# First layer's scan: high and low part of x in one 128-row operand, one selection product per tile

## The reference

```python
Bm = x @ W_B.T + b_B;  Cm = x @ W_C.T + b_C                  # 16 states
Delta = softplus(x @ W_Delta.T + b_Delta + bias_Delta)
A_bar = exp(A * Delta)                                       # [t, 256, 16]
B_bar = 1 / A * (A_bar - 1) * Bm
state = state * A_bar + x[..., None] * B_bar                 # step over t
y = sum_n state * Cm
x = layernorm(x + y)
# experts: 33 (32 routed and a shared one), each for every token
x = layernorm(x + sum_e w[t, e] * (silu(x Wg + bg) * (x Wu + bu)) Wd + ...)
```

## Time and profile before

| what | value |
|---|---|
| median of 3 runs | 3612.2 us (3611.98 to 3612.59) |
| the profiled execution's own time | 3615.77 us |
| its span in the trace | 3614.0 us |
| instructions | 44054, of these 11760 matmuls |
| matmuls in `replicate` (L360 and L361) | 2 x 256 |
| iterations with tiles and experts in all steps | 2 to 7 |
| DMA | 327.07 MB, mean 91 GB/s |

### The profile page before, as it was taken

How to read it: one execution, slowest core, us unless ns; L and a number is a source line. 1 busy time by engine, 2 the same in 40 slices (tenths; PEclk the granted TensorE clock), 3 DMA queues, 4 the chain that set the end, 5 groups by cost and what they waited for, 6 DMA issues and landing times. The chain is left out here.

```text
span 3614.0 us, 44054 instructions
## 1 busy us (share of the span) xinstructions
PE 3289.7 (91%) x11760; PEld 1691.7 (47%) x11760; DVE 2618.1 (72%) x3781; ACT 2279.7 (63%) x3238; POOL 2337.2 (65%) x1680
## 2 busy tenths in 40 slices
PE   4799999999999999998889999999986899989997
PEld 1256666666666666775333333333332333333332
DVE  5988788787877787543799999999995444444442
ACT  2366666666666666664666567566642677777786
POOL 3578787777877877773587787788772334433443
PEclk7599999999999999999899999999998899999999
DMA  1034343433433334553122222222221222222221
GB/s 70 0 101 115 106 118 108 118 107 114 116 112 111 117 111 122 146 146 83 59 70 65 68 68 66 66 69 68 66 70 44 77 99 102 97 89 95 94 94 74
DMA packets 195046, 327.07 MB, mean 91 GB/s; under 512 B 20867, under 2 KB 56868, under 8 KB 194412
## 3 DMA queue, kind: packets, MB, share of 16 engines
q1 hardware_dynamic: 194796, 324.21, 29.3%
HBM read 317.04 MB, written 7.09 MB: 90 GB/s over the span
## 5 line engine op out<-in xcount | busy, mean ns | idle before, releaser
L1432 POOL TENSOR_TENSOR c_hc<-c_h,c_c_rep 128x1024 f32<-128x1024 f32 x256 | 604.1, 2366 | 240.3 <-DVE c_h L1483 205.3
L1901 POOL TENSOR_TENSOR d_acc<-d_acc,d_prod 128x512 f32<-128x512 f32 x240 | 317.2, 1322 | 525.7 <-DVE d_prod L1969 525.3
L1483 DVE TENSOR_TENSOR_SCAN c_h<-c_decay,c_carry,c_v_ps 128x512 f32<-128x512 f32 x512 | 628.7, 1264 | 0.0
L1862 ACT ACTIVATE d_hmid<-d_up,d_b 128x1024 f32<-128x1024 f32 x512 | 541.7, 1112 | 122.9 <-PE d_up L1766 119.0
L1333 ACT ACTIVATE c_decay<-c_dt,c_a_cols 128x512 f32<-128x512 f32 x512 | 357.2, 719 | 368.7 <-DVE c_h L1483 351.2
L1183 PE MATMUL c_y_ps<-c_hc,ident 128*128 128x512 f32 x1024 | 522.4, 634 | 51.2 <-POOL c_hc L1432 44.3
L699 POOL TENSOR_TENSOR ab_inner_low<-ab_inner,ab_inner_high 128x512 fp32r<-128x512 f32 x264 | 342.0, 1295 | 297.3 <-ACT ab_inner_high L568 297.1
L557 ACT ACTIVATE ab_gate_ps<-ab_gate_ps,ab_raw_d 128x512 f32<-128x512 f32 x264 | 174.4, 660 | 510.8 <-PE ab_gate_ps L408 510.8
L1969 DVE SCALAR_TENSOR_TENSOR d_prod<-d_eo,d_b,d_w_rep 128x512 f32<-128x512 f32 x240 | 180.2, 751 | 350.1 <-PE d_eo L1776 287.2
L775 DVE SCALAR_TENSOR_TENSOR ab_tanh<-ab_tanh,ab_gate_ps 128x512 f32<-128x512 f32 x264 | 180.9, 685 | 347.8 <-ACT ab_tanh L562 346.6
L681 POOL TENSOR_TENSOR ab_hc<-ab_h,ab_c_rep 128x512 f32<-128x512 f32 x256 | 329.7, 1288 | 105.4 <-DVE ab_h L760 105.4
(11 more groups left out here) (239 smaller groups left out, 6609.4 us busy)
## 6 DMA issues: line engine op xcount, KB each, us to landing
ab_raw_gu<-in_b_experts SPq DMA_DIRECT2D x264, 256.0 KB, 3.4
...
c_c_rep<-c_c_scratch SPq DMA_DIRECT2D x256, 256.0 KB, 3.1
d_w_rep<-d_w_scratch SPq DMA_DIRECT2D x256, 256.0 KB
...
```

The lines of the kernel that those rows point to most:

```text
L1432: nc.gpsimd.tensor_tensor(hc[:, q % HC], h[:, q % HR], c_rep[:, q % BC].unsqueeze(1).broadcast_to([P, PAIR, CH]), ALU.mult).then_inc(hc_re ...
L1483: nc.vector.tensor_tensor_scan(out=h[:, q % HR, m, :], data0=decay[:, i % DEC, :], data1=v_ps[m][:], initial=carry[:, i:i + 1], op0=ALU.mu ...
L1862: nc.scalar.activation(hmid[:, (2 * q + r) % HM], up_ps[r][:], ACT.Gelu, bias=b1[:, e:e + 1]).then_inc(gelu_ready, 1)
L1901: nc.gpsimd.tensor_tensor(acc[:, s, g, :], acc[:, s, g, :], prod[:, q % PR, :], ALU.add).then_inc(add_ready, 1)
```

## The change

x of a half chunk m (128 features) is loaded anew from DRAM, in a layout of its own: `raw_x` holds the 64 rows of each half of m in partitions 0 to 63, as two slots of 512 columns, and a second copy of the same in partitions 64 to 127. ACT copies all 128 partitions and both slots to `xa` (fp32r, 128x1024 per call instead of 128x512). POOL then overwrites partitions 64 to 127 with x minus high (64x1024, in place). So 64 rows of x stand in `xa` as 64 high rows and 64 low rows, and `sel_rep`, now 8 matrices of 128 x 128 with ones in both halves, picks and adds them in one product of 128 rows. Two matmuls of 32 rows per tile become one of 128 rows.

With it: the ring of `h` has 4 tiles instead of 8. SP issues the loads of `raw_x`, two of 256 KB per half chunk, the first ahead of all constants of the layer, the second after the first expert loads, the others at steps 12 and 26; each waits for the `low_a` before. `high_a` waits for the load. `low_a` moves ahead of the expert work in POOL's steps 2 and 19, with a wait for POOL's own `weigh_state` before it and one for its own end behind it. `sel_rep` grows from 256 to 512 KB. (No other code calls `low_a` or `high_a` than what the listing shows.)

```diff
--- before.py
+++ after.py
@@ -119,7 +119,7 @@
     E1 = wb["experts"].shape[0]
     D, NE, K = 2 * P, E1 - 1, 8
     GU = 2 * D
-    REP, AB, HR, HC, RING = 2, 4, 8, 8, 3
+    REP, AB, HR, HC, RING = 2, 4, 4, 8, 3
     OFF, LAG = 23, 2
     F32R = mybir.dt.float32r
     PARTS = ((0, 0), (0, 1), (1, 0))
@@ -129,7 +129,7 @@
     Q_RES1, Q_MEAN_A, Q_CENTRE_A, Q_SQUARE_A, Q_VAR_A, Q_DEV_A, Q_SCALE_A = 3, 5, 6, 7, 8, 9, 11
     Q_LOGITS, Q_KEEP, Q_TURN, Q_AFF, Q_PICK, Q_BACK, Q_WEIGHTS, Q_STORE = 12, 13, 14, 15, 16, 18, 19, 20
     Q_PROJ, Q_SPREAD = (16, 20, 22), (17, 21, 23)
-    Q_RES0 = 19
+    Q_RES0, Q_LOAD_X = 19, (12, 26)
     Q_RES_B, Q_MEAN_B, Q_CENTRE_B, Q_SQUARE_B, Q_VAR_B, Q_LOG, Q_SCALE_B = OFF + 1, OFF + 3, OFF + 4, OFF + 5, OFF + 6, OFF + 7, OFF + 8
     ORDER = ("mean_a", "var_a", "logits", "turn", "proj0", "back", "proj1", "proj2", "mean_b", "var_b")
     with ExitStack() as ctx:
@@ -152,8 +152,10 @@
         step_bias = sb("step_bias", [P, 1])
         a_cols = sb("a_cols", [P, NT])
         inv_a = sb("inv_a", [P, NT])
-        xa = [sb(f"xa_{n}", [P, 2, CH], F32R) for n in ("high", "low")]
-        sel_rep = sb("sel_rep", [P, KPQ, P], F32R)
+        SEL = 2 * KPQ
+        raw_x = sb("raw_x", [P, 2, CH])
+        xa = sb("xa", [P, 4, CH], F32R)
+        sel_rep = sb("sel_rep", [P, SEL, P], F32R)
         b_rep = sb("b_rep", [P, 2, CH])
         c_rep = sb("c_rep", [P, 2, CH])
         step = sb("step", [P, 2, CH])
@@ -161,7 +163,7 @@
         err = sb("err", [P, CH])
         decay = sb("decay", [P, AB, CH])
         h = sb("h", [P, HR, CH])
-        sel_in = h[:, 0:KPQ * P // CH].rearrange("p a b -> p (a b)").rearrange("p (k m) -> p k m", k=KPQ)
+        sel_in = h[:, 0:SEL * P // CH].rearrange("p a b -> p (a b)").rearrange("p (k m) -> p k m", k=SEL)
         carry = sb("carry", [P, NT])
         hc = sb("hc", [P, HC, CH])
         za, zb, zc = sb("za", [P, 2, CH]), sb("zb", [P, 2, CH]), sb("zc", [P, 2, CH])
@@ -189,6 +191,7 @@
 
         loaded = sem("loaded")
         const_ready = sem("const_ready")
+        x_loaded = sem("x_loaded")
         xa_high = sem("xa_high")
         xa_low = sem("xa_low")
         work_ready = sem("work_ready")
@@ -280,6 +283,14 @@
 
         @block.sync
         def _(sp):
+            def load_x(c, m):
+                if positive(c * 2 + m):
+                    sp.wait_ge(xa_low, c * 2 + m)
+                x = wa["x"].rearrange("(m h p) t -> m p h t", h=2, p=P // 2)[m, :, :, cols(c)]
+                for half in range(2):
+                    sp.dma_start(raw_x[half * P // 2:(half + 1) * P // 2], x).then_inc(x_loaded, 16)
+
+            load_x(0, 0)
             sp.dma_start(sel_in, wa["sel_rep"]).then_inc(loaded, 16)
             sp.dma_start(w_bc[:], wa["w_bc"].rearrange("(h p) c m -> p h c m", p=P)).then_inc(loaded, 16)
             sp.dma_start(bias[:, 0:1], wa["b_b"]).then_inc(loaded, 16)
@@ -319,6 +330,8 @@
                 for n in range(STEPS):
                     if n == Q_STORE and has(i, "back"):
                         store_weights(i, s)
+                    if n in Q_LOAD_X and has(i, "proj0"):
+                        load_x(i + 1, Q_LOAD_X.index(n))
                     g = expert_at(i, n)
                     if valid(g + 4) and positive(g + 2):
                         load_gu(g + 4, (n + 4 - OFF) % E1)
@@ -333,6 +346,7 @@
             for e in range(RING):
                 load_gu(e, e)
                 load_dn(e, e)
+            load_x(0, 1)
             over_chunks(sp, NCH, lambda c, s, first, last: iteration(c, s))
             iteration(NCH, 0)
             iteration(NCH + 1, 1)
@@ -356,10 +370,8 @@
                 if n % TPB == 0:
                     pe.wait_ge(xa_low, c * 2 + m + 1)
                 pe.wait_ge(h_ready, c * NT + n + 1 + AB - REP)
-                q = slice(QUAD * j, QUAD * j + QUAD)
-                nc.tensor.matmul(rep_ps[n % REP][:], sel_rep[q, kk, :], xa[0][q, m, :], start=True, stop=False)
-                nc.tensor.matmul(rep_ps[n % REP][:], sel_rep[q, kk, :], xa[1][q, m, :], start=False,
-                                 stop=True).then_inc(rep_ready, 1)
+                nc.tensor.matmul(rep_ps[n % REP][:], sel_rep[:, j % 2 * KPQ + kk, :], xa[:, 2 * m + j // 2, :],
+                                 start=True, stop=True).then_inc(rep_ready, 1)
 
             def add_states(c, n):
                 m, kk, j = n // TPB, n % TPB // NQ, n % NQ
@@ -530,11 +542,10 @@
                 nc.scalar.activation(e_abs[:], e_abs[:], ACT.Ln, bias=1.0).then_inc(soft, 1)
 
             def high_a(c, m):
-                if is_int(c, 2) and m == 0:
-                    act.wait_ge(k["rest_loaded"], 16)
+                act.wait_ge(x_loaded, (c * 2 + m + 1) * 32)
                 if positive(c):
                     act.wait_ge(rep_ready, (c - 1) * NT + TPB * (m + 1))
-                nc.scalar.copy(xa[0][:, m], xT[:, m, cols(c)]).then_inc(xa_high, 1)
+                nc.scalar.copy(xa[:, 2 * m:2 * m + 2, :], raw_x[:]).then_inc(xa_high, 1)
 
             def split_gu(i, n, g):
                 slot = (n - OFF) % RING
@@ -671,9 +682,12 @@
                 nc.gpsimd.tensor_tensor(step[:, s, :], step[:, s, :], e_abs[:], ALU.add).then_inc(step_part, 1)
 
             def low_a(c, m):
+
                 pool.wait_ge(xa_high, c * 2 + m + 1)
-                nc.gpsimd.tensor_tensor(xa[1][:, m], xT[:, m, cols(c)], xa[0][:, m].bitcast(F32), ALU.subtract
+                rows, of = slice(P // 2, P), slice(2 * m, 2 * m + 2)
+                nc.gpsimd.tensor_tensor(xa[rows, of, :], raw_x[rows], xa[rows, of, :].bitcast(F32), ALU.subtract
                                         ).then_inc(xa_low, 1)
+                pool.wait_ge(xa_low, c * 2 + m + 1)
 
             def weigh_state(c, s, n):
                 pool.wait_ge(h_ready, c * NT + n + 1 + AB)
@@ -704,21 +718,23 @@
                     g = expert_at(i, n)
                     if n >= 1 and below(i, NCH):
                         weigh_state(i, s, n - 1)
+                    if n == 2 and below(i, NCH):
+                        pool.wait_ge(hc_ready, i * NT + n + HR)
+                        low_a(i, 1)
+                    if n == Q_SPREAD[0] + 2 and has(i, "proj0"):
+                        pool.wait_ge(hc_ready, i * NT + n + HR)
+                        low_a(i + 1, 0)
                     if valid(g - 1):
                         split_inner((n - 1 - OFF) % E1, g - 1)
                     if valid(g + 2):
                         split_gu(n + 2, g + 2)
                     if valid(g):
                         split_dn(n, g)
-                    if n == 2 and below(i, NCH):
-                        low_a(i, 1)
                     if n == Q_LOGITS + 1 and has(i, "logits"):
                         pool.wait_ge(xb_high, i)
                         nc.gpsimd.tensor_tensor(xb[1][:, 1 - s], xT[:, :, cols(i - 1)],
                                                 xb[0][:, 1 - s].bitcast(F32), ALU.subtract).then_inc(xb_low, 1)
                     if has(i, "proj0"):
-                        if n == Q_SPREAD[0] + 2:
-                            low_a(i + 1, 0)
                         if n == Q_SPREAD[2] + 2:
                             find_error(i + 1)
                         if n == Q_SPREAD[2] + 3:
@@ -2080,7 +2096,7 @@
                         sp.dma_start(ident[:], d["ident"]).then_inc(loaded, 16)
                         sp.dma_start(xT[:, :, 2 * CH:], x[:, :, 2 * CH:]).then_inc(rest_loaded, 16)
                         sp.wait_ge(loaded, 4 * 16)
-                layer0(nc, xT, k, {n[2:]: a for n, a in d.items() if n.startswith("a_")},
+                layer0(nc, xT, k, {"x": d["xT"], **{n[2:]: a for n, a in d.items() if n.startswith("a_")}},
                        {n[2:]: a for n, a in d.items() if n.startswith("b_")}, weights)
             layer1_scan(nc, xT, k, of_scan, weights)
         layer1_experts(nc, xT, k, {n[2:]: a for n, a in d.items() if n.startswith("d_")})
@@ -2104,10 +2120,12 @@
         return a.reshape(-1, P).T
 
     row = np.arange(P)
-    sel_rep = np.zeros((P, KPQ, P), np.float32)
+    sel_rep = np.zeros((P, 2 * KPQ, P), np.float32)
     sel_sum = np.zeros((P, KPQ, QUAD), np.float32)
     for kk in range(KPQ):
-        sel_rep[:, kk, :] = (row[:, None] % QUAD) == (row[None, :] // N_STATE + DPT * kk)
+        for j in range(2):
+            sel_rep[:, j * KPQ + kk, :] = ((row[:, None] % (2 * QUAD))
+                                           == (row[None, :] // N_STATE + DPT * kk + QUAD * j))
         sel_sum[:, kk, :] = (row[:, None] // N_STATE + DPT * kk) == np.arange(QUAD)[None, :]
 
     sel_parts = np.zeros((P, NQ, 2, P), np.float32)
```

## The result

| what | before | after |
|---|---|---|
| median of the runs | 3612.1 us (3611.5 to 3612.6) | 3571.7 us (3570.4 to 3576.6) |
| ratio, with its 95% interval | | 0.9886 [0.9871, 0.9901] |
| span of the profiled execution | 3614.0 us | 3569.8 us |
| first scan of the first layer | 38.0 us | 41.1 us |
| last scan of the first layer | 1415.0 us | 1379.5 us |

The change makes the kernel 1.1% faster, 40.4 us by the medians; forecast was 3571 us. The table says where the 44.2 us between the two spans come from. The stretch from the first scan to the last gives 1377.0 - 1338.4 = 38.6, the start takes 3.1 away, the experts that are left after the last scan give 4.9, and the second layer the remaining 3.8. The last two run through code that the change doesn't touch; what they are worth is told with the experiments.

What follows compares the result with a forecast made beforehand. PE was taken to set the pace, with 0.47 us in hand before the ACT and DVE path. Terms -41 - 1.6 + 2 = -41 against 3615.8 gave 3575, the median 3.6 lower: 3571 us, range 3525 to 3603.

Steps and rivals of the forecast that it cites:

- The saving of 0.63 us a tile: PE's replication: one matmul of 0.23 us and both changes of shape go in 32 of 33 steps, 20.2 us a chunk.
- What is given back: Of PE's relief of 20.2 us a chunk, 13.3 come back as waits; net 6.9, a chunk of 188.0 us.
- Where it is given back: Ten plain steps wait for weigh, 5.5 us in all; PE's wait before up rises from 4 us to some 60 or more.
- the equation for u(n+1): Start of up in the next step: later of g(n+1) + 1.59 and end of weigh(n) + 0.16 us.
- The ring: Ring of h, 8 to 4 tiles: POOL is less than two steps late, three are allowed; costs nothing.
- POOL's longer subtraction: POOL's steps 2 and 19: the subtraction takes 2.43 us, 1.14 more, twice a chunk, covered by idle time; costs nothing.
- The loads: Raw x loads, 1 MB a chunk on queues 40% busy, issued five steps ahead of use; cost nothing.
- The start: Before the first scan: 512 KB of raw x and 256 KB more selectors delay PE by 2 us, bounds 0.9 and 3.
- A (PE alone, 3487): Rival: PE alone sets the pace, so all 20.2 us a chunk come through, 3487 us; chance 0.13.
- C (gaps stay, 3586): Rival: gaps around replication come from waits, not shape, and stay; 4.5 us a chunk gained, 3586 us; chance 0.12.
- D (given back whole): Rival: longer POOL and ACT jobs or later loads fall on the deciding path, 3605 to 3619 us; chance 0.09.
- E (the clock): Rival: more PE idle time lowers its granted clock to 0.95, making the kernel slower, about 3627 us; chance 0.09.

Runs made afterwards that it cites:

- Experiment 2: The kernel before with the low product left out, one 32-row matmul per tile with both changes of shape kept; 3588.9 us, ratio 0.9926.
- Experiment 1: The changed kernel with the replication product issued twice per tile into the same bank; 3583.5 us, ratio 0.991.
- Experiments 6: The changed kernel with DVE's driving and scan both moved ahead of gated; 3554.5 us, ratio 0.9833.
- 8: The kernel before with DVE's driving and scan both moved ahead of gated; 3612.5 us, ratio 0.9988.
- experiment 3: The kernel before with the ring of h cut from 8 tiles to 4 and nothing else; 3616.7 us, ratio 1.0.
- experiment 4: The changed kernel with POOL's subtraction put back behind the expert work of steps 2 and 19; 3577.0 us, ratio 0.9887.
- experiment 10: The changed kernel with the scan's three DVE instructions one tile ahead, woven between those of the expert; 3670.3 us, ratio 1.015.
- numbers 5: The changed kernel with only DVE's driving moved ahead of gated; 3583.0 us, ratio 0.9908.
- Number 9: The changed kernel with DVE's order driving, scan, gated, scaled of the next tile, product, weigh; 3543.4 us, ratio 0.9789.

## Why the prediction was right

**The saving of 0.63 us a tile.** Right: 0.23 and 0.24 us around the new product, a free step of 4.33 us where 4.34 was forecast. Experiment 2 shows that the gaps go with the 32-row shape; with one product gone and the shape kept, over a third of the gain is missing (14.1 of 38.4 us). The rule on changing the tiling mode (the Trainium skill, "TensorEngine Tiling (Array Packing)", Key Properties) agrees with these runs: 0.43 us at a change between 128 and 32 rows, 0.23 without one.

**What is given back.** Right in size: 188.0 us forecast for a chunk, 188.48 measured, so 6.2 gained and not 20.2. Experiment 1 shows it without the arithmetic: another matmul per tile, 46 us beside the experts, costs 6.9. Experiments 6 and 8 show whose path took it.

**Where it is given back.** Only half right. The forecast had every new wait at `up`, some 60 us or more, all for `weigh`. The profile has two places: the replication, which waits for the scan two tiles back, and `up`. In the first step of the timeline 0.38 us are lost at the first (0.61 instead of 0.23), 0.35 at the second, and 0.11 for the weight load that is exposed by the wait. The step of the prediction that failed is the equation for u(n+1): it had weigh's end, but not the scan's. What the runs showed in its place: before the replication PE and its loads wait 33.5 and 71.1 us for scans, before `up` 7.6 and 48.4 for `weigh`. I take it that the sum was spared because scan and `weigh` are neighbours on DVE and late together, so that the wait at the replication uses up time that `up` would have waited; a run with a third replication bank, which would take the first wait away, was not made. Nor did I read the load's rows: PEld waited 48 us for scans before the change already, so the room was thinner than the 4 us in the earlier trace rows suggest.

**The terms at nothing.** The ring: right, by experiment 3. POOL's longer subtraction: it took 2.40 us, the upper of the two near rows as I chose, and experiment 4 shows that its place costs nothing. The loads: no wait for raw x appears between 200 and 1400 us, and DMA is busy for 0.43 of the chunk instead of 0.40.

**The start.** The term was 2, its upper bound 3, the measurement 3.1 us: a mis-sized term. I had counted bytes and two issues of 0.45; the issues took 1.38, and another 2.58, so that PE began 4.9 us later, and an earlier rise of the clock gave back 1.8. That rise differs from run to run, and it moves the first scan by as much as the load's place does.

**The sum.** Iterations 2 to 7 gained 37.0 us, 6.2 each, and the scans before them 1.7; the table has 38.6 for both. The forecast had 6.9 for each and 1.6 and so 42.6, against which stand 3.1 lost at the start instead of 2: 35.5 us gained where 40.6 were forecast. The code that isn't touched, forecast at nothing, gave the missing 5 and 3.7 more in the profiled execution; on the other side the 3.6 us that I took off for the median were not there after the change. So 3571 is closer to the median than its parts are to theirs, and that is luck.

**The rivals.** A (PE alone, 3487): refuted by experiment 1. C (gaps stay, 3586): by experiment 2 and the timeline. D (given back whole): the chunk is 6.2 us shorter. E (the clock): granted 1.00 in 1200 to 1400 us. The idea behind E was not idle, though: in experiment 10 the clock is 0.97. One of its stretches, one of PE's waits in it, and 3.2 us that follow that wait:
```profile
200.00:400.00 200.00, 177.79 (x728) 123.63 (x729) 160.58 (x237) 126.44 (x224) 159.09 (x140) 0.97 0.41 117
...
318.63 0.50 PE L432 MATMUL ab_up_ps<-ab_xb_high,ab_gu_high 128*128 128x512 f32 x1 [4.04 <-DVE ab_inner L808]
...
319.10:322.30 3.20, 3.20 (x9) 2.47 (x8) 2.94 (x5) 1.58 (x4) 2.92 (x3) 0.50 0.17 42
```
In 200 to 1400 us PE stands idle for 3.2 to 4.0 us 17 times in experiment 10, and at each of these the clock falls to 0.50; five more falls come where PE had stood idle for at most 2.2 us, and numbers 5, 6 and 9 have three to five falls, beside idle times of 1.4 to 2.5, and once of 4.5. In the kernel after PE's longest idle time between 204 and 1400 us is 1.9 us, and there is no fall.

The rule that spoke against the change (the Trainium skill, "TensorE: Matmul & The Clock Gate", A second HAM failure mode: psum-queue depth-cycling) did not take effect at the waits of the kernel after, where the granted clock of 1200 to 1400 us is 1.00. In experiment 10 most falls stand beside one long wait; whether that mode has a part in the other five, no run here separates.

**The experiments' own misses.** Numbers 5 and 6 were worked out with DVE as a queue of busy times, without the 0.12 to 0.18 us that a reader comes later behind its result; no run shows that this is the whole of their 38 and 39 us. Number 10 was worked out without ACT's decay. Number 9 is 18 us short of what was expected, and most of it is accounted for: the stretch before the experts is 18.2 longer than forecast, 11.8 of which are waits of `scaled` for the replication, the one beside them 2.9 shorter; the last 3 us fit code that isn't touched.
